# A recurrent mixing layer on one core: one ScalarE table set for Ln and Exp, preloaded, and four dummies less

## The reference

```
xn  = ln(x);  sx = shift(xn) - xn
xxx = tanh((xn + sx*maa_x) @ maa_w1) @ maa_w2          # five mixes
x5  = xn + sx * (maa_stack + xxx)
w   = exp(-exp(time_decay + tanh(x5[1] @ decay_w1) @ decay_w2))
r, k, v = x5[3] @ Wr.T, x5[0] @ Wk.T, x5[2] @ Wv.T;  g = silu(x5[4] @ Wg.T)
s_t = k_t v_t + w_t * s_(t-1);  out_t = r_t (u k_t v_t + s_(t-1))
att = (out - mean) * rsqrt(var + eps) * gn_w + gn_b     # per head of 8
x   = x + (att * g) @ Wo.T
xn2 = ln(x);  xk, xr = mixes of xn2 and its shift
x   = x + sigmoid(xr @ Fr.T) * (square(relu(xk @ Fk.T)) @ Fv.T)
```

## Time and profile before

| | |
|---|---|
| runs (us) | 1242.73, 509.7, 507.69 (median 509.7) |
| profiled execution | 507.84 us, of which the span 506.0 us |
| granted clock of PE, mean | 0.993 |
| PE busy | 475.6 us (94%) |
| DVE busy | 467.0 us (92%) |
| ACT busy | 281.4 us (56%) |
| POOL busy | 89.6 us (18%) |

### The profile page before, as it was taken

How to read it: one execution, slowest core, us unless ns; L and a number is a source line. 1 busy time by engine, 2 the same in 40 slices (tenths; PEclk the granted TensorE clock), 3 DMA queues, 4 the chain that set the end, 5 groups by cost and what they waited for, 6 DMA issues and landing times. The chain is left out here.

```text
span 506.0 us, 6206 instructions
## 1 busy us (share of the span) xinstructions
PE 475.6 (94%) x2172; PEld 277.4 (55%) x2172; DVE 467.0 (92%) x521; ACT 281.4 (56%) x611; POOL 89.6 (18%) x100
## 2 busy tenths in 40 slices
PE   3788899999999999999999999999999999988797
PEld 2564545655446347544556456644655556556476
DVE  3779898999999999999999999999999999998665
ACT  2354666477546834777447764563558463455343
POOL 0101003210610051011401051003130231203020
PEclk9899999999999999999999999999999999999999
DMA  8365685597869576993789664884869477905031
GB/s 272 123 161 114 169 173 104 116 211 162 149 174 230 123 122 157 213 204 63 133 200 223 133 124 111 212 207 81 181 139 211 79 113 178 217 2 114 0 40 34
DMA packets 28136, 73.03 MB, mean 144 GB/s; under 512 B 1737, under 2 KB 20297, under 8 KB 25673
## 3 DMA queue, kind: packets, MB, share of 16 engines
q1 hardware_dynamic: 19720, 54.68, 44.2%
q0 software_dynamic: 8384, 17.96, 21.2%
HBM read 46.28 MB, written 12.19 MB: 116 GB/s over the span
## 5 line engine op out<-in xcount | busy, mean ns | idle before, releaser
L624 DVE TENSOR_TENSOR_SCAN kv<-w_sb,kv 128x512 f32<-128x512 f32 (+2 forms) x144 | 146.9, 1083 | 0.9 <-ACT w_sb L859 0.6
L952 PE MATMUL pa<-x,large_sb 128*128 128x512 f32 (+2 forms) x272 | 115.2, 567 | 4.6 <-DVE x L539 3.9
L952 PEld LDWEIGHTS pa<-x,large_sb 128*128 128x128 f32 x272 | 51.0, 194 | 60.3 <-issue 47.5
L632 DVE TENSOR_TENSOR kv<-kv,r_sb 128x2048 f32<-128x2048 f32 (+2 forms) x36 | 73.5, 2045 | 0.3
L614 DVE TENSOR_TENSOR kv<-vrep,k_sb 128x2016 f32<-128x2016 f32 (+2 forms) x34 | 70.1, 2061 | 1.1 <-PE patt L1124 1.1
L445 POOL COPY kv<-s_sb 128x32 f32<-128x32 f32 (+2 forms) x36 | 30.0, 837 | 157.4 <-PE patt L1124 145.4
L414 POOL DMA_DIRECT2D x<-xn x28 | 28.2, 1008 | 145.9 <-DVE x L530 145.5
L530 DVE SCALAR_TENSOR_TENSOR x<-pb,vec_sb,sx 128x512 f32<-128x512 f32 (+1 forms) x64 | 42.7, 708 | 2.4 <-PE pb L1030 1.4
L1124 PE MATMUL patt<-kv,const_sb 128*32 128x512 f32 (+2 forms) x288 | 33.7, 555 | 0.0
L996 PE MATMUL pb<-th,w_sb 32*128 32x512 f32 (+2 forms) x100 | 33.4, 597 | 0.0
L1164 PE MATMUL pc<-large_sb,att 128*128 128x256 f32 x120 | 28.2, 386 | 2.2 <-DVE att L648 2.2
(11 more groups left out here) (187 smaller groups left out, 806.6 us busy)
## 6 DMA issues: line engine op xcount, KB each, us to landing
vrep<-v_scratch SPq DMA_DIRECT2D x12, 2048.0 KB, 15.7
x<-xn POOLq DMA_DIRECT2D x24, 512.0 KB, 5.7
vrep<-v_scratch SPq DMA_DIRECT2D x4, 1536.0 KB, 12.7
x_tok<-in_x SPq DMA_DIRECT2D x6, 512.0 KB, 10.0
v_scratch<-v_sb SPq DMA_DIRECT2D x12, 256.0 KB
xres<-in_x SPq DMA_DIRECT2D x6, 512.0 KB, 4.5
out<-xres SPq DMA_DIRECT2D x6, 512.0 KB, 10.1
out<-trr POOLq DMA_DIRECT2D x6, 512.0 KB, 9.1
```

Of the source, the lines that this page charges most:

```text
L624: ins = dve.tensor_tensor_scan(flat, w_sb[:, p, q % HF, 0:nb].rearrange("p b t -> p (b t)"), flat, 0.0, ALU.mult, ALU.add)
L632: dve.tensor_tensor(flat, flat, r_sb[:, p, q % HF:q % HF + 1, 0:n].broadcast_to([P, G4, n]), ALU.mult).then_inc(rs_ready, 1)
L952: ins = pe.matmul(dst[:, m, 0:n], w(a)[:, m * P:(m + 1) * P], src[:, a, :], start=(a == 0), stop=(a == HF - 1))
```

## The change

The set `natural_log_exp_and_others`, which has Ln and Exp, is loaded by hand: at the start of every `a_w`, ahead of its waits; at `c_rstd` of chunk 0; and at `c_sq` of the last chunk, ahead of its wait. Behind the last `c_rstd` a set with Tanh is loaded. The compiler then adds loads only where a function is missing from the set at hand. Of the six dummies ahead of the wo step of the last chunk two remain.

```diff
--- before.py
+++ after.py
@@ -12,6 +12,7 @@
 S = E // H
 LORA, DECAY = 32, 64
 EPS = 1e-5
+LN_EXP = "natural_log_exp_and_others"
 ROOT = 16
 assert ROOT * ROOT == E
 P = 128
@@ -87,7 +88,7 @@
     sx2.4 lr.5 vl1.6 sx2.5 lr.6 vst.7 vl0.7 vl1.7 vst.8 sx2.6 lr.7 vl0.8 vl1.8 sx2.7 lr.8 sx2.8
 """
 WARM = {("KK", 1): 6, ("RR", 7): 5, ("RR", 9): 1, ("T1", 0): 2, ("T2", 2): 6, ("T2", 3): 6, ("T2", 4): 6,
-        ("T2", 5): 6, ("T2", 6): 6, ("T2", 7): 14, ("T2", 9): 3, ("W1", 0): 1, ("WO", 0): 6, ("WO", 8): 6,
+        ("T2", 5): 6, ("T2", 6): 6, ("T2", 7): 14, ("T2", 9): 3, ("W1", 0): 1, ("WO", 0): 6, ("WO", 8): 2,
         ("X01", 0): 2}
 ADDED = (0, 1, 3, 4)
 MIXED = {0: 1, 1: 2, 2: 3, 3: 4, 4: 5}
@@ -844,6 +845,7 @@
 
             def a_w(c, p):
 
+                act.preload_act_table_set(LN_EXP)
                 act.wait_ge(d2_done, c + 1)
                 if c >= 1:
                     act.wait_ge(w_ready, c)
@@ -869,6 +871,8 @@
                 act.activation(sg[:, p, :, 0:n], pa[:, :, 0:n], ACT.Silu).then_inc(sg_ready, 1)
 
             def c_sq(c, p):
+                if c == LAST:
+                    act.preload_act_table_set(LN_EXP)
                 act.wait_ge(summed, NQ * (c + 1))
                 if c >= 1 and c != LAST:
                     act.wait_ge(y2_done, c)
@@ -876,6 +880,8 @@
                 act.activation(squares(c)[:, :, 0:n], patt[:, :, 0:n], ACT.Square).then_inc(sq_ready, 1)
 
             def c_rstd(c, p):
+                if c == 0:
+                    act.preload_act_table_set(LN_EXP)
                 act.wait_ge(var_done, c + 1)
                 if c >= 1:
                     act.wait_ge(scaled, c)
@@ -883,6 +889,8 @@
                 act.activation(rstd[:, 0:n], product(c)[:, 1, 0:n], ACT.Ln, bias=eps_sb[:, 0:1]).then_inc(ln_ready, 1)
                 act.wait_ge(ln_ready, c + 1)
                 act.activation(rstd[:, 0:n], rstd[:, 0:n], ACT.Exp, scale=-0.5).then_inc(rstd_ready, 1)
+                if c == LAST:
+                    act.preload_act_table(ACT.Tanh)
 
             def c_xn(k, _):
                 act.wait_ge(t2_done, k + 1)
```

## The result

The changed kernel is slower by a little: 509.77 us (median of 20 runs, 508.63 to 512.96) against 508.44 of before, in 20 runs on the same chips. The ratio is 1.0039 with a 95% interval of 1.0023 to 1.0054, so about +2.0 us. The medians lie only 1.3 us apart; the ratio is that of the means, and 8 of the 20 runs of the changed kernel form a group of their own at 510.5 to 513 us, which lifts its mean to 510.40. Single runs far above all others, such as 1242.73 us of before, are left out of every ratio. The profiled execution took 509.44 us with a span of 507.6.

A forecast was written before the change was run, and what follows sets the result against it. DVE and PE, almost without gaps from 120 to 450 us, were taken as the bound, so only waits for ACT count: 507.84 us profiled, +1.4 + 2.1 - 1.7 = +1.8, gives 509.6; range 506.0 to 512.5.

The forecast's parts named there:

- The sum: Whole kernel: +1.4 + 2.1 - 1.7 = +1.8 us, put on the profiled 507.84 us, giving 509.6.
- The middle: Middle chunks: fourteen table loads removed at the roots, hidden behind DVE's work, so worth 0.
- the cover: Middle chunks: DVE takes the root late, behind a scan, so 3.9 us of ACT time is hidden.
- The first decay: Chunk 0, w.0: a load added between xhat and the first Exp, with nothing covering it; +1.4 us.
- both legs: Chunk 0: DVE's first scan and PE's projection for r both move by the same 1.4 us.
- The third decay: Loads added at rr.0 and w.2 make DVE's mix wait for w_sb; +2.1 us.
- Carried to the end undiminished: After 112 us DVE has no gaps, so both early delays reach the end whole: +3.5 us.
- The last root: Last chunk: two loads leave the path, two dummies remain, the last product with Wo starts earlier; -1.7 us.
- Absorbed at the start: Rival, chance 0.20: gaps at the start take up the 3.5 us, only the end counts; 506.1 us.
- ACT counts after all: Rival, chance 0.03: late ACT steps set DVE's pace, up to 15.4 us come off; 492.4 us.
- Clock at the end: Rival, chance 0.03: fewer dummies let PE's clock fall to 1.2 GHz at about 485 us; 518.6 us.
- Clock at the start: Rival, chance 0.14: longer PE gaps at 31 and 100 us bring one or two clock dips; 511.3 to 513.

The follow-up runs named there:

- Three loads more: Kernel before with three more table loads between Ln and Exp of the root in each of chunks 3 to 7; ratio 1.0317 to before.
- the undoing: Changed kernel without the added table load ahead of the decay of chunk 0; ratio 0.9996 to before.
- the two undoings: Changed kernel without the load at w.0, 0.9996 to before; separately, changed kernel without the loads at rr.0 and w.2, 1.0004 to before.
- the tail alone: Kernel before with only the last root's table loads moved and two dummies instead of six; all middle loads kept; ratio 0.9976 to before.
- one load more: Kernel before with one more table load between Ln and Exp of the root in each of chunks 3 to 7; ratio 1.0009 to before.

## Why the prediction was right or wrong

**The number.** 509.6 was forecast and 509.77 measured; the difference to before, +1.8 forecast, was +2.0. That the two times agree to 0.2 us is partly luck: the base of 507.84 was 0.6 us below the median of before, and the median of the changed kernel is 0.6 us below its mean. And the same 509.6 lies 0.1 us below the 509.7 that was the median of the three runs shown of before, and read against that it says "no change", while the kernel is slower, clear of the noise (1.0023 at the lower end). The step that failed is the last one of "The sum": I saw that the runs shown were three with an outlier, and still gave a number on the profiled execution's scale and left the difference to be read off against another one. What the runs showed in its place: over 20 runs before is 508.44, not 509.7; on that scale my sum would have been 510.2. The chance of 0.94 for "within 2%" was right, and too coarse to say what I had worked out.

**The middle** (loads removed that nobody waits for: 0). Right in its result: D to E is 368.84 with these loads and without. Wrong in the cover: 3.9 us was the distance to a wait that is not the nearest. Three loads more, 3.85 us, should have been hidden and cost 16 us. The nearest who waits is PE, for Tanh, with 1.8 us of cover, and each chunk without a dip paid the other 2.0. I had looked at who waits for the root itself, not at what stands behind it in ACT's queue. The second cover had no part in the sum, since the change only took loads away here.

**The first decay** (+1.4). Measured 1.44 between the marks and 1.43 in the undoing; both legs moved, as written.

**The third decay** (+2.1). Measured 2.31. DVE's waits show it in pieces: 1.61 us at the mix instead of 0.19, 0.36 at rk of chunk 2 and 0.38 at the output of chunk 1, which both had been tight. I had counted the PE step that is 0.8 us late, and summed at the mix alone; what is missing, 0.2 us, comes back later: D to E is 0.1 to 0.2 us shorter in all kernels with these loads. "Carried to the end undiminished" holds to that extent.

**The last root** (-1.7). Measured -1.72. The condition that PE's dummies set, and that with six of them nothing would be gained, came out as written.

**The rivals.** Absorbed at the start (0.20): false for both terms, by the two undoings. ACT counts after all (0.03): false, by the tail alone and by one load more. Clock at the end (0.03): false, even with no dummies. Clock at the start (0.14): a dip came in one of four profiles with the late load of w.0 (1.65 us), though not in the changed kernel's own, and the runs show it more often with that load than without (17 of 56 against 13 of 186). So this rival is real as an addition, and the forecast, which has nothing for it, is short by a few tenths of a us in the mean. The dip in 72:80 was priced at 8 x 0.21 = 1.7 us and is worth 0.72 to 0.74; that row doesn't show the gaps of PE that are said to stand ahead of it either. What I did not see is the other side: the profile before had such a dip and the changed kernel's had none, while the latter started 0.40 us later. So the profiles' difference is 1.58 - 0.40 + 0.72 = 1.90 us without both, beside the sum of 1.8.

**The price of a load.** It is 1.29 to 1.30 us in all these rows, whichever sets are changed, and back to back as well (227.16, 228.45): no drain. The Trainium skill ("ScalarE: Activation LUTs", What ACT_TABLE_LOAD costs) would have put the three exposed loads at twice that, with its 2.66 us for a switch. The trace doesn't agree, and the measurement decides.

## What to carry to other kernels

A preload gains only where the engine would stand idle in the wait that it is moved ahead of; on an engine that arrives late it is a plain addition, and a set chosen for two functions can lack a third that the old one had. Count loads by who stands still behind each, following the whole queue behind them, not only the next use of the result: here 14 removed were worth nothing, three added cost 3.7 us, and two removed gained 1.7 only together with four dummies less (0 without that). And when the effect is 1 us in 500, set marks in the trace and compare stretches between profiles. Where engines did the same and the clock was the same, most stretches repeated to 0.01 us while the runs of one kernel scattered by 4, and the few that didn't were told apart by a dip or by one stop of DVE.

## What the runs showed of the hardware

- The start scatters: DVE's first product k v stood between 27.26 and 29.96 us in 14 profiles of kernels that are the same up to there but for one, and all that follows is moved with it. That is as large as the whole effect of this change. It goes with the granted clock of the first 30 us: 27.26 in the one profile with 1.00, 27.94 to 29.31 in the eight with 0.94, 29.14 to 29.96 in the five with 0.89.
- The granted clock dips in some executions and not in others of the same program. At 32 us it did so in one profile of the changed kernel (0.79 in 32:40) and not in the other two, worth 1.65 us. In 72:80 it did so in the profile before and in two others (0.79), worth 0.72 to 0.74 us. In the kernel with three loads more it stood at 0.79, 0.72 and 0.60 over 8, 12 and 8 us, the first time right behind a wait of PE of 1.94 us for Tanh.
- Sets with different functions load in the same 1283 ns, and loads back to back start 1.29 us apart.
